# The delta-rule layer's turned keys: products of 32 rows in place of 64-row products over a two-head copy

## The chip, the cores and the metric

The kernel runs on one core of one Trainium2 chip, in float32. The metric is the device time of one launch in microseconds (us). Engines: TensorE (PE, with its weight loads as PEld), VectorE (DVE), ScalarE (ACT), GpSimd (POOL), and SyncE (SP), which here only issues DMAs.

## The reference

The reference is four transformer-like layers, one after the other (attention, gated delta rule, retention, a linear recurrence, each followed by a mixture of experts). The change is in the second one, the delta rule over 8 sequences of 256 tokens. The width of 128 is 4 heads of 32, and the tokens are taken in chunks of 32. What the change touches, cut to its core:

```python
q = silu(causal_dwconv(hidden @ Wq, wq_conv))      # likewise k and v; 4 taps
q, k = l2norm(q), l2norm(k)
v, kb = v * beta[..., None], k * beta[..., None]
# everything in chunks of 32 tokens, per head
inv = -(kb @ swap(k)) * strict_lower
for i in range(1, chunk):
    inv = inv.at[..., i, :].add(einsum('...j,...jk->...k', inv[..., i, :], inv))
inv = inv + eye(chunk)
u, w = inv @ v, inv @ kb
def step(S, xs):                                     # chunk after chunk
    qi, ki, ui, wi = xs
    attn = qi @ swap(ki) * lower_incl
    ui2 = ui - wi @ S
    oi = qi @ S + attn @ ui2
    return S + swap(ki) @ ui2, oi
```

Then come two FIR filters of the values, a gate over the four branches, a norm and an output projection.

## The kernel before

Each layer is a block of its own; inside a block every engine has an instruction list written out by hand in program order, and semaphores ("tallies", `wait_ge` and `then_inc`) set what waits for what. The delta layer is `delta_scan` followed by `delta_gate`. Its data lie as 128 partitions, which are 4 heads times 32, by 2048 columns, which are 8 sequences (b) times 8 chunks (n) times 32; a (b, n) pair is a unit, 64 in all. `kT` holds the turned keys (dimension of the head on partitions, token in columns), `qT` the queries, `kH` the keys turned back, in 32 by 32 blocks.

**Two forms of product.** A product of one head needs only a 32 by 32 block of weights. `products` issues it so, dense: one matmul for each of the 4 heads, on partitions `head(h)`, 32 for a chunk of the 8 sequences. `pair_products` issues it with two heads side by side: the weights are 64 by 64, on partitions `two_heads(i)`, and the two blocks off the diagonal must be zero, so 16 matmuls do for a chunk. Such weights are a copy with the head index e spread out (`kT_heads`, and `inverse`). The copies are made by ScalarE with a scale per partition from `heads` (1 for the heads of parity e, 0 for the others). In the trace every float32 matmul is two records of weight load and two of product.

**The order of `delta_scan`**, by engine:

1. TensorE: gate projection; the convolution of k (`convolve(2, ...)`, 4 groups g of 512 columns into psB); then `pairs(psA, f["kT"], g)`, the products of keys with keys, for the 4 groups; convolutions of v, transposes of windows, the filters, the convolution of q; `pairs(psB, f["qT"], g)`, queries with keys.
2. ScalarE in this phase: for g = 0..3 `silu(0, ...)` writes kT from psB, two more activations write `kT_heads` from psB and signal `split`, then the square of kH of the group before; the fifth turn squares the last group, and a square root follows.
3. VectorE: turns kT into kH by groups, sums the squares (`ssk`), works out the factors `G`, `rk`, `rt`, multiplies psA by `G` (L2757), turns it (L2763), and runs the inversion of the 32 by 32 triangles as 31 pairs of instructions (L2768, L2772). Then it turns the result into r3 (L2786), from which ScalarE makes the two-head copy `inverse` (L2632).
4. The scan over n = 0..7. TensorE: K = keys times state into psK (n above 0), O = queries times state into psO, U = inverse times r into psU, S = kH times u2 into psS, A = attention block times u2 into psO. VectorE: r = vb minus K (L2846), state plus S (L2861); ScalarE copies psU to u2 (L2693). Between these VectorE does side work in program order: evictions of O (`evict`, L2805), the statistics sums, `turn_filtered` at n = 2 and 3 (L2797), `short_sums` at n = 5, 6, 7. I call the steps step 0 to step 7.

Then `delta_gate` begins with a chain of TensorE products (L3044 to L3058).

Of the kernel before, what the change touches and what calls it, by code (L numbers as in the profile page):

```python
# [8 lines left out]
ACT = mybir.ActivationFunctionType  # L9
AX = mybir.AxisListType  # L10

P = 128
# [2333 lines left out]
CH = 32  # L2346
DHEADS = D // CH
UN = N // CH
CPS = SEQ // CH
# [86 lines left out]
def delta_scan(k, f, vpad, w, windows, raw, small, one, sums, r2, r3):  # L2436

    nc = k.nc
    w_in = k.tally("df_w_in")
    scaled, made, convd, silud, spread, moved, fired, firs_in = (  # L2440
        k.tally(f"df_{n}") for n in ("scaled", "made", "convd", "silud", "turned", "moved", "fired", "firs_in"))
# [3 lines left out]
    carried, copied, less, solved, solved_out, read, added, out_done = (  # L2445
        k.tally(f"dt_{n}") for n in ("carried", "copied", "less", "solved", "solved_out", "read", "added", "out_done"))
    cols, rows = w["cols"], w["rows"]
    cleared, cons = k.tally("df_raw_read"), k.tally("dg_cons")
    split, inverted, powered, vsummed, dsquared, dsummed = (
        k.tally(f"ds_{n}") for n in ("split", "inverted", "powered", "vsummed", "dsquared", "dsummed"))  # L2450
    inverse = windows[:].rearrange("p n c -> p (n c)").rearrange("p (u e c) -> p u e c", e=2, c=CH)
    unit_heads = lambda t, b, n, i: t[2 * CH * i:2 * CH * (i + 1), b * CPS + n, :, :].rearrange("p e c -> p (e c)")
    wc = w["conv"][:].rearrange("p (i j c) -> p i j c", i=3, c=D)
    seqs = lambda t: t.rearrange("p (b s) -> p b s", s=SEQ)
    H = lambda ap: ap.rearrange("p (u d) -> p u d", d=CH)
# [4 lines left out]
    head = lambda h: slice(CH * h, CH * (h + 1))  # L2460
    two_heads = lambda i: slice(2 * CH * i, 2 * CH * (i + 1))
    unit = lambda b, n: slice((b * CPS + n) * CH, (b * CPS + n + 1) * CH)
    with ExitStack() as s:
        sb = lambda n, shape: s.enter_context(nc.sbuf_tensor(f"ds_{n}", shape, F32))
        incl, heads = sb("incl", [P, CH]), sb("heads", [P, 2])
        kT_heads = sb("kT_heads", [P, UN, 2, CH])
        tmp = sb("tmp", [P, 2, CH * CH // 4 + CH])
        state, r, u2 = (sb(n, [P, BATCH, CH]) for n in ("state", "r", "u2"))
        squares = tmp[:].rearrange("p g c -> p (g c)")[:, 0:2 * BATCH * CH].rearrange("p (i b c) -> p i b c", i=2, c=CH)
# [48 lines left out]
        @block.tensor  # L2518
        def _(pe):
            def convolve(i, ps, g):  # L2520
                out, x = seqs(ps[:, g, :]), seqs(part(k.XT, g))
                for late in range(CONV):
                    m = nc.tensor.matmul(out[:, :, late:], wc[:, i, CONV - 1 - late, :], x[:, :, 0:SEQ - late],
                                         start=(late == 0), stop=(late == CONV - 1))
                m.then_inc(convd.sem, 1)

            def pairs(out, right, q):
                for b in (2 * q, 2 * q + 1):
                    for n in range(CPS):
                        for i in range(2):  # L2530
                            m = nc.tensor.matmul(
                                out[two_heads(i), q, (b % 2 * CPS + n) * CH:(b % 2 * CPS + n + 1) * CH],
                                unit_heads(kT_heads, b, n, i), right[two_heads(i), unit(b, n)],
                                start=True, stop=True)
                m.then_inc(multiplied.sem, 1)

            def spread_windows(ps, b):
                for j in range(4):
                    m = nc.tensor.transpose(ps[:, b % 4, j * P:(j + 1) * P], vpad[:, b, LONG * j:LONG * j + P],
                                            k.ident[:])  # L2540
                m.then_inc(spread.sem, 1)

            def filter_half(ps, half):
                for d in range(16 * half, 16 * half + 16):
                    for h in range(DHEADS):
                        m = nc.tensor.matmul(ps[CH * h:CH * (h + 1), d % 16 // 4, d % 4 * P:(d % 4 + 1) * P],
                                             windows[:, :, CH * h + d], k.firs[:, d, h, :], start=True, stop=True)
                m.then_inc(fired.sem, 1)

            def pair_products(out, left, n, right):  # L2550
                for b in range(BATCH):
                    for i in range(2):
                        m = nc.tensor.matmul(out[two_heads(i), b * CH:(b + 1) * CH], unit_heads(left, b, n, i),
                                             right[two_heads(i), b, :], start=b == 0, stop=True,
                                             skip_group_check=True)
                return m

            def products(out, left, n, right, start=None, stop=True):
                for b in range(BATCH):
                    for h in range(DHEADS):  # L2560
                        m = nc.tensor.matmul(out[head(h), b * CH:(b + 1) * CH], left[head(h), unit(b, n)],
                                             right[head(h), b, :], start=b == 0 if start is None else start, stop=stop,
                                             skip_group_check=True)
                return m

            pe.wait_ge(*w_in.at(16 * DELTA_LOADS))
            for g in range(4):
                m = nc.tensor.matmul(psA[:, g, :], w["Wxg"][:], part(k.XT, g), start=True, stop=True)
            m.then_inc(gates.sem, 1)
            pe.wait_ge(*scaled.at(1))  # L2570
            for g in range(4):
                convolve(2, psB, g)
            pe.wait_ge(*gout.at(1))
            for g in range(4):
                pe.wait_ge(*split.at(g + 1))
                pairs(psA, f["kT"], g)

            pe.wait_ge(*scaled.at(2))
            convolve(0, psB, 0)
            convolve(0, psB, 1)  # L2580
            pe.wait_ge(*opened.at(4))
            for g in (0, 1):
                if g:
                    convolve(0, psB, 2)
                pe.wait_ge(*silud.at(4 + g + 1))
                spread_windows(psA, 2 * g)
                spread_windows(psA, 2 * g + 1)
            convolve(0, psB, 3)
            for g in (2, 3):
                pe.wait_ge(*silud.at(4 + g + 1))  # L2590
                spread_windows(psB, 2 * g)
                spread_windows(psB, 2 * g + 1)
            pe.wait_ge(*firs_in.at(64))
            pe.wait_ge(*moved.at(8))
            filter_half(psA, 0)
            filter_half(psB, 1)

            pe.wait_ge(*scaled.at(3))
            pe.wait_ge(*kept.at(1))
            for g in range(4):  # L2600
                convolve(1, psA, g)
            pe.wait_ge(*kept.at(2))
            for g in range(4):
                pe.wait_ge(*silud.at(8 + g + 1))
                pairs(psB, f["qT"], g)

            for n in range(CPS):
                if n:
                    pe.wait_ge(*added.at(n))
                    pair_products(psK, kT_heads, n, state).then_inc(carried.sem, 1)  # L2610
                    if n > 1:
                        pe.wait_ge(*copied.at(n - 1))
                    products(psO[n % 2], f["qT"], n, state, stop=False)
                pe.wait_ge(*split.at(4 + n + 1))
                pe.wait_ge(*less.at(n + 1))
                pair_products(psU, inverse, n, r if n else at(f["vb"], 0)).then_inc(solved.sem, 1)
                pe.wait_ge(*solved_out.at(n + 1))
                if n < CPS - 1:
                    products(psS, f["kH"], n, u2).then_inc(read.sem, 1)
                if n == 0:  # L2620
                    pe.wait_ge(*opened.at(8))
                products(psO[n % 2], f["attn"], n, u2, start=False if n else None).then_inc(out_done.sem, 1)

        @block.scalar
        def _(act):
# [23 lines left out]
            for g in range(5):  # L2649
                if g < 4:  # L2650
                    silu(0, seqs(part(f["kT"], g)), psB, g)
                    for e in range(2):
                        m = nc.scalar.activation(kT_heads[:, 16 * g:16 * g + 16, e, :], H(psB[:, g, :]), ACT.Silu,
                                                 scale=heads[:, e:e + 1])
                    m.then_inc(split.sem, 1)
                if g:
                    act.wait_ge(*turned.at(1 + g))
                    nc.scalar.activation(part(r3, g - 1), part(f["kH"], g - 1), ACT.Square).then_inc(squared.sem, 1)
# [219 lines left out]
            output_sums(CPS - 1)  # L2878
    gates.close(1); gout.close(1); turned.close(5); squared.close(8); made.close(2)
    rooted.close(2); asked.close(2); sig.close(1)  # L2880
    split.close(4 + CPS); inverted.close(2); cleared.close(1); powered.close(14)
    vsummed.close(1); dsquared.close(CPS - 1); dsummed.close(CPS)


# [633 lines left out]
```

## Time and profile before

| | |
|---|---|
| median of 3 runs | 1330.14 us (1330.45, 1330.14, 1320.05) |
| profiled execution | 1328.31 us, of which its span is 1326.6 us |
| granted TensorE clock, mean | 0.894 |
| PE, PEld, DVE, ACT, POOL busy | 1098.2, 804.9, 800.2, 534.7, 377.4 us |
| `delta_scan` in that span | about 345 to 483 us |
| `delta_gate` | about 483 to 552 us |

Busy shares are means over all layers; the two stretches of the delta layer are read by themselves. The granted clock is a share of TensorE's full rate of 2.4 GHz; in any one moment it is 1.0 or 0.5 (1.2 GHz). A matmul's own duration is its latency; how densely matmuls follow one another is read from when the first and the last of a group start.

### The profile page before, as it was taken

The numbers are of one execution on the slowest core, as the hardware profiler recorded it, in microseconds if no ns is written. First come the engines' busy times: TensorE is split into PE (matmuls) and PEld (weight loads), VectorE is DVE, ScalarE is ACT, GpSimd is POOL, SyncE is SP. The second block draws the span as 40 slices with busy tenths as digits, with TensorE's granted clock in tenths as the row PEclk, the third lists the DMA queues.
The fourth block names the chain that finished last, engine by engine and source line by source line (L and its number), as shares of the span: only waits on it lengthen the run. The fifth ranks groups of instructions, "written<-read, shape, count | busy, mean of one in ns | idle before, by whom it ended". The sixth has DMA issues, their size and how long they took to land. (4 is left out here: it accounts for less than half of the span.)

```text
span 1326.6 us, 28735 instructions
## 1 busy us (share of the span) xinstructions
PE 1098.2 (83%) x9623; PEld 804.9 (61%) x9631; DVE 800.2 (60%) x2789; ACT 534.7 (40%) x1167; POOL 377.4 (28%) x515
## 2 busy tenths in 40 slices
PE   8999887884998883789976858886878989899892
PEld 4655555674466851446644414553756979889791
DVE  6566245344588669635566785556962767767423
ACT  4365632474553331222222113332213656658481
POOL 2444405343101530000000014660024444534351
PEclk9899978898998566899987976998987999999996
DMA  1200439222000049049917064652902212031212
GB/s 48 55 33 3 152 132 381 62 65 76 1 2 2 4 151 367 1 114 184 318 53 258 2 211 123 147 141 68 362 25 69 70 35 69 22 72 43 62 47 64
DMA packets 112895, 135.88 MB, mean 102 GB/s; under 512 B 16899, under 2 KB 78422, under 8 KB 112096
## 3 DMA queue, kind: packets, MB, share of 16 engines
q1 hardware_dynamic: 100160, 119.26, 29.1%
q0 software_dynamic: 12592, 14.79, 4.4%
q8 instruction: 80, 1.31, 0.4%
q14 instruction: 63, 0.52, 0.1%
HBM read 67.92 MB, written 69.32 MB: 103 GB/s over the span
## 5 line engine op out<-in xcount | busy, mean ns | idle before, releaser
L2116 PE MATMUL m_psY<-large,m_hT 128*128 (+2 forms) x992 | 139.2, 284 | 0.0
L2116 PEld LDWEIGHTS m_psY<-large,m_hT 128*128 128x128 f32 x992 | 126.7, 191 | 0.1
L2035 POOL DMA_INDIRECT rows<-m_ys,m_slot x93 | 90.7, 975 | 113.6 <-DVE m_slot L2271 102.9
L567 DVE TENSOR_REDUCE at_peaks<-at_ps 128x3 f32<-128x384 f32 x128 | 65.4, 552 | 47.6 <-PE at_ps L330 47.6
L479 ACT ACTIVATE at_PT<-at_ps,at_bias 128x384 f32<-128x384 f32 x128 | 67.3, 577 | 50.2 <-PE at_ps L340 50.1
L2172 ACT ACTIVATE m_hT<-m_psH 128x512 f32<-128x512 f32 x124 | 73.7, 594 | 30.1 <-PE m_psH L2098 29.7
L1480 POOL IOTA sl_late<- 64x1024 f32 x2 | 2.0, 984 | 284.8 <-POOLq L682 284.7
L126 PE MATMUL ln_idle<-blank,ident 128*128 128x512 f32 x112 | 54.1, 640 | 27.5 <-PEq L891 14.8
L274 POOL TENSOR_SCALAR_AFFINE_SELECT at_PT<-at_PT 128x256 f32<-128x256 f32 x128 | 54.9, 430 | 74.0 <-ACT at_PT L479 70.0
L2098 PE MATMUL m_psH<-m_xT,large 128*128 128x128 f32 x512 | 67.6, 275 | 0.0
L2184 ACT ACTIVATE m_ys<-m_psY,m_weight 128x144 f32<-128x144 f32 x124 | 47.3, 381 | 42.7 <-PE m_psY L2116 38.3
L2098 PE MATMUL m_psH<-m_xT,m_up 128*128 128x128 f32 x480 | 63.7, 276 | 0.0
L2098 PEld LDWEIGHTS m_psH<-m_xT,large 128*128 128x128 f32 x512 | 63.5, 194 | 0.0
L2098 PEld LDWEIGHTS m_psH<-m_xT,m_up 128*128 128x128 f32 x480 | 59.8, 195 | 0.0
L126 PEld LDWEIGHTS ln_idle<-blank,ident 128*128 128x128 f32 x112 | 22.4, 206 | 54.8 <-issue 54.8
L1377 ACT ACTIVATE pe_sg<-pe_psG 128x512 f32<-128x512 f32 x36 | 21.5, 597 | 69.6 <-PE pe_psU L1345 69.6
L2165 ACT ACTIVATE m_xT<-m_psX 128x128 f32<-128x128 f32 x124 | 32.8, 264 | 41.0 <-PE m_psX L2085 41.0
L1047 PE MATMUL m_psH<-m_xT,m_up 128*128 128x128 f32 x280 | 41.7, 295 | 8.8 <-issue 8.4
L327 PE MATMUL at_ps<-large,at_QA 32*128 32x256 f32 x256 | 46.0, 433 | 3.4 <-ACT at_PT L479 2.3
L1353 PEld LDWEIGHTS pe_psD<-m_wd,pe_hid 128*128 128x128 f32 x288 | 37.5, 191 | 18.5 <-DVE pe_hid L1398 13.8
L981 POOL DMA_INDIRECT pair_sums<-m_ys,m_dest x35 | 34.4, 983 | 44.2 <-ACT m_ys L1106 30.8
L337 PE MATMUL at_ps<-at_QA,large 32*128 32x256 f32 x256 | 44.8, 425 | 2.5 <-ACT at_PT L479 2.3
(709 smaller groups left out, 2780.5 us busy)
## 6 DMA issues: line engine op xcount, KB each, us to landing
rows<-blank SPq DMA_DIRECT2D x16, 2448.0 KB, 21.0
m_xs<-rows SPq DMA_DIRECT2D x124, 76.5 KB, 2.0
pair_rows<-blank SPq DMA_DIRECT2D x1, 8320.0 KB, 25.7
large<-in_L_attn_firs SPq DMA_DIRECT2D x4, 2048.0 KB, 19.1
large<-comb_rows SPq DMA_DIRECT2D x64, 128.0 KB, 5.1
se_wu<-in_L_ffn_up SPq DMA_DIRECT2D x32, 192.0 KB, 2.6
W2T<-in_L_ffn_down_turned SPq DMA_DIRECT2D x1, 4096.0 KB, 12.3
large<-in_L_ffn_up SPq DMA_DIRECT2D x4, 1024.0 KB, 8.2
```

Of the source, the lines that this page charges most:

```text
L126: nc.tensor.matmul(idle[:], k.ident[:], k.blank[:, 0:512], start=True, stop=True)
L274: nc.gpsimd.affine_select(out=diag(PT[:, v % PRING]), in_=diag(PT[:, v % PRING]), compare_op=ALU.is_ge, fill=0.0, base=0, pattern=[[0, 2], ...
L327: return nc.tensor.matmul(psS[:, u % TILES, P:CAUSAL], QA[rows, g, keys(b, 1)], KA[rows, g, b * SEQ:(b + 1) * SEQ], start=False, stop=True ...
L337: return nc.tensor.matmul(psT[:, v % TRING, 0:SEQ], KA[rows, g, keys(b, 0)], QA[rows, g, b * SEQ:(b + 1) * SEQ], start=True, stop=True, sk ...
L479: nc.scalar.activation(PT[:, v % PRING, :, :].rearrange("p x c -> p (x c)"), psT[:, v % TRING, 0:CAUSAL], ACT.Exp, bias=k.at_bias[:, v % H ...
L567: nc.vector.tensor_reduce(peaks[:, b % 2, n, :], psS[:, u % TILES, 0:CAUSAL].rearrange("p (x c) -> p x c", c=P), AX.X, ALU.max).then_inc(r ...
L1047: m = nc.tensor.matmul(psH[b][:, c * P:(c + 1) * P], up[b][:, c * P:(c + 1) * P], xT[b][:], start=True, stop=True)
L2035: pool.indirect_dma_start(k.rows[(layer + 1) % 2], bass.IndirectOffsetOnAxis(slot[:, q:q + 1], 0), ys[:, q, :], None, bounds_check=E3 * N ...
L2098: m = nc.tensor.matmul(psH[b][:, c * P:(c + 1) * P], w[:, c * P:(c + 1) * P], xT[b][:], start=True, stop=True)
L2116: m = nc.tensor.matmul(psY[b][:, 0:wide], hT[b][:, c * P:(c + 1) * P], w, start=(c == 0), stop=(c == C - 1))
L2172: nc.scalar.activation(hT[b][:], psH[b][:], ACT.Silu).then_inc(silu_done.sem, 1)
L2184: nc.scalar.activation(ys[:, q, 0:WIDE], psY[b][:, 0:WIDE], ACT.Copy, scale=weight[:, j % XRING:j % XRING + 1]).then_inc(y_out.sem, 1)
```

## The change

`kT_heads` is given up, with the 8 activations that filled it. Three users change. `pairs` issues, for each unit, 4 matmuls of 32 by 32 weights straight from kT in place of 2 of 64 by 64: 256 in place of 128, twice. Step K of the scan uses `products` in place of `pair_products`: 32 matmuls in place of 16, in 7 steps. And `pairs` on the keys waits for `silud`, the signal of kT itself, not for `split`. The inverse stays two heads side by side. The outputs lie where they lay, and the sums over a head have the same 32 terms (the 64-row form added 32 products with zero).

```diff
--- before.py
+++ after.py
@@ -2463,7 +2463,6 @@
     with ExitStack() as s:
         sb = lambda n, shape: s.enter_context(nc.sbuf_tensor(f"ds_{n}", shape, F32))
         incl, heads = sb("incl", [P, CH]), sb("heads", [P, 2])
-        kT_heads = sb("kT_heads", [P, UN, 2, CH])
         tmp = sb("tmp", [P, 2, CH * CH // 4 + CH])
         state, r, u2 = (sb(n, [P, BATCH, CH]) for n in ("state", "r", "u2"))
         squares = tmp[:].rearrange("p g c -> p (g c)")[:, 0:2 * BATCH * CH].rearrange("p (i b c) -> p i b c", i=2, c=CH)
@@ -2527,11 +2526,10 @@
             def pairs(out, right, q):
                 for b in (2 * q, 2 * q + 1):
                     for n in range(CPS):
-                        for i in range(2):
+                        for h in range(DHEADS):
                             m = nc.tensor.matmul(
-                                out[two_heads(i), q, (b % 2 * CPS + n) * CH:(b % 2 * CPS + n + 1) * CH],
-                                unit_heads(kT_heads, b, n, i), right[two_heads(i), unit(b, n)],
-                                start=True, stop=True)
+                                out[head(h), q, (b % 2 * CPS + n) * CH:(b % 2 * CPS + n + 1) * CH],
+                                f["kT"][head(h), unit(b, n)], right[head(h), unit(b, n)], start=True, stop=True)
                 m.then_inc(multiplied.sem, 1)
 
             def spread_windows(ps, b):
@@ -2572,7 +2570,7 @@
                 convolve(2, psB, g)
             pe.wait_ge(*gout.at(1))
             for g in range(4):
-                pe.wait_ge(*split.at(g + 1))
+                pe.wait_ge(*silud.at(g + 1))
                 pairs(psA, f["kT"], g)
 
             pe.wait_ge(*scaled.at(2))
@@ -2607,11 +2605,11 @@
             for n in range(CPS):
                 if n:
                     pe.wait_ge(*added.at(n))
-                    pair_products(psK, kT_heads, n, state).then_inc(carried.sem, 1)
+                    products(psK, f["kT"], n, state).then_inc(carried.sem, 1)
                     if n > 1:
                         pe.wait_ge(*copied.at(n - 1))
                     products(psO[n % 2], f["qT"], n, state, stop=False)
-                pe.wait_ge(*split.at(4 + n + 1))
+                pe.wait_ge(*split.at(n + 1))
                 pe.wait_ge(*less.at(n + 1))
                 pair_products(psU, inverse, n, r if n else at(f["vb"], 0)).then_inc(solved.sem, 1)
                 pe.wait_ge(*solved_out.at(n + 1))
@@ -2649,10 +2647,6 @@
             for g in range(5):
                 if g < 4:
                     silu(0, seqs(part(f["kT"], g)), psB, g)
-                    for e in range(2):
-                        m = nc.scalar.activation(kT_heads[:, 16 * g:16 * g + 16, e, :], H(psB[:, g, :]), ACT.Silu,
-                                                 scale=heads[:, e:e + 1])
-                    m.then_inc(split.sem, 1)
                 if g:
                     act.wait_ge(*turned.at(1 + g))
                     nc.scalar.activation(part(r3, g - 1), part(f["kH"], g - 1), ACT.Square).then_inc(squared.sem, 1)
@@ -2878,7 +2872,7 @@
             output_sums(CPS - 1)
     gates.close(1); gout.close(1); turned.close(5); squared.close(8); made.close(2)
     rooted.close(2); asked.close(2); sig.close(1)
-    split.close(4 + CPS); inverted.close(2); cleared.close(1); powered.close(14)
+    split.close(CPS); inverted.close(2); cleared.close(1); powered.close(14)
     vsummed.close(1); dsquared.close(CPS - 1); dsummed.close(CPS)
 
 
```

On TensorE, from the products of keys with keys (`pairs` into psA) the row before the change and the one after:

```order
L2531 MATMUL ds_psA<-de_kT,ds_kT_heads 64x32 x128
```

```order
L2530 MATMUL ds_psA<-de_kT 32x32 x256
```

Nothing around this row is in another place; its count doubles and its weights come from kT. On TensorE the first rows of steps 1 and 2 of the scan, in the order K, O, U, S, A, first before:

```order
L2553 MATMUL ds_psA<-ds_state,ds_kT_heads 64x32 x16
L2561 MATMUL ds_psB<-ds_state,large 32x32 x32
L2553 MATMUL ds_psA<-ds_r,de_windows 64x32 x16
L2561 MATMUL ds_psA<-ds_u,de_kH 32x32 x32
L2561 MATMUL ds_psB<-ds_u,large 32x32 x32
L2553 MATMUL ds_psA<-ds_state,ds_kT_heads 64x32 x16
```

and after:

```order
L2559 MATMUL ds_psA<-ds_state,de_kT 32x32 x32
L2559 MATMUL ds_psB<-ds_state,large 32x32 x32
L2551 MATMUL ds_psA<-ds_r,de_windows 64x32 x16
L2559 MATMUL ds_psA<-ds_u,de_kH 32x32 x32
L2559 MATMUL ds_psB<-ds_u,large 32x32 x32
L2559 MATMUL ds_psA<-ds_state,de_kT 32x32 x32
```

The order stands; K has the form of O, S and A, and only U has the 64-row form. On ScalarE, the end of the key groups (from the kT of g = 2), before:

```order
L2628 ACTIVATE de_kT<-ds_psB 128x512
L2653 ACTIVATE ds_kT_heads<-ds_psB,ds_heads 128x16x32 x2
L2658 ACTIVATE de_r<-de_kH 128x512
L2628 ACTIVATE de_kT<-ds_psB 128x512
L2653 ACTIVATE ds_kT_heads<-ds_psB,ds_heads 128x16x32 x2
L2658 ACTIVATE de_r<-de_kH 128x512 x2
```

and after:

```order
L2626 ACTIVATE de_kT<-ds_psB 128x512
L2652 ACTIVATE de_r<-de_kH 128x512
L2626 ACTIVATE de_kT<-ds_psB 128x512
L2652 ACTIVATE de_r<-de_kH 128x512 x2
```

The squares now come right behind the writes of kT. VectorE's, GpSimd's and SyncE's lists are the same.

## Rows read from the trace of the kernel before

**Rows 1.** Busy time and granted clock (PEclk) of stretches: products with keys, scan, gate

```profile
core 0: us, PE busy (x) PEld busy (x) DVE busy (x) ACT busy (x) POOL busy (x), PEclk, DMA share, GB/s
362.50:370.00 7.50, 7.50 (x257) 7.49 (x256) 5.02 (x15) 7.21 (x12) 0.00 (x0) 1.00 0.01 2
...
419.60:420.00 0.40, 0.40 (x16) 0.40 (x16) 0.40 (x2) 0.40 (x2) 0.00 (x0) 1.00 0.00 0
...
423.40:482.00 58.60, 46.66 (x1735) 43.78 (x1728) 43.58 (x95) 19.26 (x38) 32.03 (x31) 0.50 0.01 4
483.00:488.00 5.00, 5.00 (x6) 2.15 (x7) 4.67 (x9) 1.67 (x2) 0.00 (x0) 0.50 0.78 283
488.50:497.00 8.50, 8.50 (x21) 3.72 (x20) 1.43 (x2) 4.03 (x5) 0.00 (x0) 1.00 1.03 372
```

**Rows 2.** Timeline from the last key group to the inversion (start, us, engine, line)

```profile
362.51 7.66 PE L2531 MATMUL ds_psA<-de_kT,ds_kT_heads 64*64 64x32 f32 x256
362.62 0.60 ACT L2628 ACTIVATE de_kT<-ds_psB 128x512 f32<-128x512 f32 x1 [1.14 <-PE ds_psB L2523]
363.11 1.26 ACT L2653 ACTIVATE ds_kT_heads<-ds_psB,ds_heads 128x512 f32<-128x512 f32 x2
363.25 0.71 DVE L2733 STREAM_TRANSPOSE de_kH<-de_kT 128x512 f32<-128x512 f32 x1 [1.05 <-ACT de_kT L2628]
364.25 1.16 ACT L2658 ACTIVATE de_r<-de_kH 128x512 f32<-128x512 f32 x2
...
365.53 0.68 DVE L2738 TENSOR_REDUCE de_ssk<-de_r 128x16 f32<-128x512 f32 x1
...
369.86 1.28 DVE L2757 TENSOR_TENSOR de_r<-ds_psA,de_G 128x512 f32<-128x512 f32 x2
...
373.13 1.25 DVE L2757 TENSOR_TENSOR de_r<-ds_psA,de_G 128x512 f32<-128x512 f32 x2
```

**Rows 3.** Timeline from the products of queries with keys to step 0

```profile
409.52 7.66 PE L2531 MATMUL ds_psB<-large,ds_kT_heads 64*64 64x32 f32 x256
...
414.90 3.67 DVE L2786 STREAM_TRANSPOSE de_r<-de_T 128x2048 f32<-128x2048 f32 x1
...
419.56 1.51 PE L2553 MATMUL ds_psA<-large,de_windows 64*64 64x32 f32 x32 [2.39 <-ACT de_windows L2632]
421.11 0.37 ACT L2693 COPY ds_u<-ds_psA 128x256 f32<-128x256 f32 x1 [0.80 <-PE ds_psA L2553]
...
421.54 1.08 PE L2561 MATMUL ds_psA<-ds_u,de_kH 32*32 32x32 f32 x64 [0.47 <-ACT ds_u L2693]
...
422.41 1.06 PE L2561 MATMUL ds_psA<-ds_u,large 32*32 32x32 f32 x64
```

**Rows 4.** Timeline of steps 2 and 3, where VectorE comes last

```profile
436.36 1.07 PE L2561 MATMUL ds_psA<-ds_state,large 32*32 32x32 f32 x64 [0.22 <-DVE large L2805]
...
441.24 3.71 DVE L2797 STREAM_TRANSPOSE large<-de_raw 128x1024 f32<-128x1024 f32 x2
...
444.81 0.39 DVE L2846 TENSOR_TENSOR ds_r<-large,ds_psA 128x256 f32<-128x256 f32 x1
```

**Rows 5.** Timeline of step 5: state, K, O, r, U

```profile
456.82 0.42 DVE L2861 TENSOR_TENSOR ds_state<-ds_state,ds_psA 128x256 f32<-128x256 f32 x1 [2.06 <-PE ds_psA L2561]
...
457.54 1.92 PE L2553 MATMUL ds_psA<-ds_state,ds_kT_heads 64*64 64x32 f32 x32
...
459.39 1.07 PE L2561 MATMUL ds_psB<-ds_state,large 32*32 32x32 f32 x64
459.50 0.42 DVE L2846 TENSOR_TENSOR ds_r<-large,ds_psA 128x256 f32<-128x256 f32 x1 [2.26 <-PE ds_psA L2553]
...
460.39 1.92 PE L2553 MATMUL ds_psA<-ds_r,de_windows 64*64 64x32 f32 x32
```

**Rows 6.** Timeline of step 6 (A's last records) and of step 7's r

```profile
464.85 0.42 PE L2561 MATMUL ds_psB<-ds_u,large 32*32 32x32 f32 x11 [0.25 <-issue]
...
475.02 0.42 DVE L2846 TENSOR_TENSOR ds_r<-large,ds_psA 128x256 f32<-128x256 f32 x1
```

**Rows 7.** Timeline of the gate: what VectorE waits for

```profile
495.37 3.29 DVE L2946 STREAM_TRANSPOSE de_T<-dg_psL 128x512 f32<-128x512 f32 x4 [7.47 <-PE dg_psL L3058]
```

## The prediction

> **What bounds the kernel now.** The table of busy time names TensorE first, but it is a mean over all the layers, and the chain that ended last reaches back only over the last norm, so neither prices this change. I read three other views: the timeline of the delta layer, engine by engine, for what ends last before each step; the waits written behind the rows; and the windows, for the granted clock. The delta layer lies alone in its block, about 345 to 483 us for the scan, and the gate behind it starts only when it is done, so what it gains or loses at its end goes into the total one for one.
>
> Inside it the chain changes hands. From the last key group on it is VectorE's: squares, factors, multiplication of psA, inversion [rows 2], then the turning of the inverse [rows 3]. TensorE's 256 records of keys with keys run from 362.51 to 370.17, and VectorE takes psA at 369.86 after a chain of its own; there is no wait for a product on that row [rows 2]. Step 0 waits for the turned inverse and its copy: TensorE idles 2.39 us before it [rows 3]. In the scan the chain is state, K, r, U, S, state, with VectorE's side work in between. Every clock row from 423.4 to 482 reads 0.5, where the rows of the two dense product groups before it read 1.0 [rows 1].
>
> **The products of 32 rows, one by one.** In the half-clock stretch, K has 32 records and takes 459.39 minus 457.54 = 1.85 us to the start of the next group, 58 ns for each [rows 5]. A dense group has 64 records for the same work: S to A in step 0 is 422.41 minus 421.54 = 0.87 us, 14 ns each [rows 3]. In step 5, O to U is 460.39 minus 459.39 = 1.00 us [rows 5], of which I put the 0.13 above 0.87 down to the change of form. So four small products flow in the time in which one large one does, and twice as many records still take half the time. At full clock, 256 records of the 64-row form take 7.5 us, 29 ns each, half of 58 [rows 1]; the 32-row form is not shown there. Its bounds are 14 ns (nothing gained from the clock) and 7 ns (halved as the large form is), so 512 records take 3.6 to 7.2 us in place of 7.6. I take the middle, 5 us.
>
> One rule speaks against this. The Trainium skill (TensorE: Matmul & The Clock Gate, "Wait — 56ns, not 53.3ns?") says that start to start never falls below about 25 ns however small the matmul. By it a dense K would take 64 times 25 = 1.6 us, and a group of 512 would take 12.8 us. The trace's 14 ns on tiles of 32 by 32 is below that floor, so for tiles on different rows of the array the measurement decides.
>
> **Keys, first part.** Removed: 8 activations, in pairs of 1.26 us [rows 2]. Three pairs lie before the last kT, while TensorE's convolution of the last group ends only at 362.6, so they were covered; ScalarE even waited 1.14 us for it [rows 2]. The last pair is not. Now: kT 362.62 to 363.22, pair to 364.37, two squares to 365.41, last sum at 365.53. After: the square of g = 2 starts at 363.1; the last square needs kH of g = 3, which VectorE turns from 363.25 to 363.96 [rows 2], so it runs from about 364.03 to 364.65, and the last sum starts at about 364.7. Gain **0.83 us**, not 1.26, because the turning is late next. The rest of VectorE's chain to 369.86 is as before. It would now meet psA at 369.0; the products of the first group are then done at any of the bounds (362.5 plus 7.2 is 369.7 even for the last group, which is needed at 372.3 [rows 2]). The square root's function load on ScalarE moves with the squares.
>
> TensorE is done with the keys 2.6 us sooner (5 us in place of 7.6; 0.4 to 4 by the bounds). What follows there, convolutions, windows, filters, queries with keys, is not the last wait of anything: it ends at 417.2, 2.39 us before step 0 [rows 3]. It costs and brings nothing by itself; the queries' products end at about 409.5 minus 2.6 plus 5 = 412. The inversion has VectorE alone, and starts and ends 0.83 us sooner, r3 at about 417.7 in place of 418.6.
>
> **Step 0, a loss.** TensorE now idles some 6.8 us before U of step 0, in place of 2.39. The clock is still 1.0 at 419.6 to 420.0 [rows 1], so the first half of U ran full; 1.51 us in all, where U at half clock takes 1.92 [rows 3, 5]. After the longer idle time I expect it at half from the start: **0.41 us lost**, with 0 as the other end. No run shows the idle time at which it falls.
>
> **Steps 1 to 4, nothing.** Step 2: O waits for VectorE's eviction, not for K, and starts at 436.36; r follows that same eviction, and U follows both [rows 4]. Steps 3 and 4: `turn_filtered` holds VectorE for 3.71 us from 441.24, and r comes at 444.81, straight behind it, with no wait for K; step 4 repeats it [rows 4]. Step 1 has the turning of the values in the same place. K sooner by 1 us meets a busy VectorE in all four.
>
> **Steps 5 and 6, the gain.** Here VectorE waits: 2.26 us before r of step 5 [rows 5]. Now: state done at 457.24, K 457.54, O 459.39, U 460.39. After: A's last records are followed by K in the same form, so K starts at about 457.37; K 0.87, O 1.00, U at 459.24. r starts at 457.37 plus about 1.1 = 458.5 and is done by 458.9, before U. Gain **1.15 us**. Step 6 has the same form, with K and O giving 0.98 back for certain; its A has a gap in issue with 11 records after it at 464.85 [rows 6] that delays K today and may go or grow (0 to 0.5 us either way): **1.0 us**. Step 7: `short_sums` keep VectorE busy right up to r at 475.02, on which no wait is written [rows 6], so it only moves with the others. From there VectorE's sums and the last eviction are the chain to the end.
>
> **The gate.** It starts earlier and is TensorE's: VectorE waits 7.47 us for its products [rows 7]. The clock there was 0.5 up to 488 and 1.0 from 488.5 [rows 1], some 5.2 us after its first product. If it rises as late after the start, nothing changes; a microsecond sooner or later is worth 0.5 us. I take 0, with 0.8 either way.
>
> **Sum.** 0.83 minus 0.41 plus 1.15 plus 1.0 = 2.6 us sooner; with the ends, 1.0 to 4.2. On the profiled execution 1328.31 minus 2.6 = 1325.7; the median of the runs lies 1.8 us above that execution, so 1330.14 minus 2.6 gives **1327.5 us**. Within 1% is about what a measurement of this kernel can't tell from no change, and 2.6 us is 0.2%; one of the three runs, 10 us below the other two, shows more than that by itself.
>
> **Rivals.**
> 1. *The gain is spent before it reaches the end.* VectorE's side work or the gap in issue takes up what K gives in steps 5 and 6, as it does in steps 2 to 4. For: K, O and A are all alike now, 64 records each, so TensorE takes 576 records of weights and products where it took 512 in a step. Against: the 2.26 us wait. Then 0.83 minus 0.41 stays, about 1330 us.
> 2. *Slower: the clock rises late in the gate.* TensorE's scan is sparser now by 7 times 1 us and idles longer before. If the clock stays at half until the gate's chain ends at 495.4, the work between 488.3 and there takes twice its time, 7.1 us more. With the gains 1330.14 minus 2.6 plus 7.1 = 1334.6 us. It decides against the change when the rise is over 5.2 us later than now, relative to the start. Against: the gate's products are eight dense groups of 512 columns in both kernels.
> 3. *Spacing by product, not by tile.* If the 32-row products of `pairs` at full clock cost as much each as the 64-row ones, 29.5 ns, keys take 15.1 us, queries too, and the queries end at 409.5 plus 7.5 plus 15.1 = 432.1 where step 0 needs them at 419.6: 12.5 us lost, less 2.2 from the scan, 1340 us. Against: 14 ns in the same array at half its clock. The skill's floor of 25 ns on the same page would put the end of the queries at 409.5 plus 5.2 plus 12.8 = 427.5, some 8 us late.
> 4. *The runs lie elsewhere.* One run of before took 1320.05. If two of the runs of after do so as well, the median is about 1318, with the same mechanism.
>
> **How the numbers follow.** Forecast 0.62; rival 1 0.17; rival 2 0.08; rival 3 0.03; rival 4 0.10. The range takes in the forecast with its ends (1326 to 1329.2), rivals 1 and 4, and part of 2: 1318 to 1333 us. Faster by over 1% means below 1316.8: half of rival 4 and a little for the unforeseen, 0.07. Slower by over 1% means above 1343.4: 0.03, out of rivals 2 and 3 joined. Within 1%: 0.90.
>
> **What would show it.** In the profile after: the last sum of squares some 2.2 us after the last kT starts, not 2.9; the keys' products within 3.6 to 7.2 us; no instruction of L2757 waiting for a product; U of step 0 spread over 1.9 us; K's records 14 ns apart in the scan; in steps 5 and 6 U starting 2 us after the state is ready, not 3.1; steps 2, 3 and 4 as long as before; the scan 2 to 3 us shorter. Wrong would be: a K that takes 1.6 us or more, a granted clock of 0.5 before 410, or steps 5 and 6 as long as now.

## The result: slower by 1%, and where the time went

The changed kernel takes 1341.98 us (median of 4 runs, 1340.68 to 1345.5), the kernel before 1329.28 us (4 runs); the ratio is 1.0101, 95% interval 1.0057 to 1.0145. Forecast were 1327.5 us and a range up to 1333. The profiled execution took 1341.34 us, its span is 1339.6 us, 13.0 over the span before; the mean granted clock is 0.885.

Up to the keys' products the two traces agree to 0.1 us. These are the lines of the timeline of after that answer to [rows 2]:

```profile
362.58 2.33 PE L2530 MATMUL ds_psA<-de_kT 32*32 32x32 f32 x250
...
364.73 0.69 DVE L2732 TENSOR_REDUCE de_ssk<-de_r 128x16 f32<-128x512 f32 x1
...
366.91 1.30 PE L2530 MATMUL ds_psA<-de_kT 32*32 32x32 f32 x128 [1.99 <-issue]
...
369.07 1.28 DVE L2751 TENSOR_TENSOR de_r<-ds_psA,de_G 128x512 f32<-128x512 f32 x2
...
370.63 1.93 PE L2530 MATMUL ds_psA<-de_kT 32*32 32x32 f32 x128 [2.43 <-issue]
...
374.09 0.33 PE L2530 MATMUL ds_psA<-de_kT 32*32 32x32 f32 x6 [1.53 <-issue]
374.34 9.50 PE L2522 MATMUL ds_psB<-XT,de_conv 128*128 128x512 f32 x16
374.46 0.69 DVE L2751 TENSOR_TENSOR de_r<-ds_psA,de_G 128x512 f32<-128x512 f32 x1 [1.52 <-PE ds_psA L2530]
```

The first 250 records of product run in 2.33 us, 9 ns apart. Then TensorE stands for 2 us, with no engine named as the one it waits for ("issue"), runs exactly 128 records, stands, runs 128, stands. A record of product has a record of load beside it, so 128 of them are 256 instructions. The group ends at 374.4 where the 64-row form ended at 370.2, and VectorE, which has its factors 0.8 us sooner than before (369.07 against 369.86), waits 1.52 us for the last of them. So the inversion begins at 377.26 instead of 376.54.

The clock adds to it. Windows of after (columns as in [rows 1]):

```profile
362.60:364.90 2.30, 2.30 (x251) 2.20 (x251) 1.45 (x3) 1.93 (x4) 0.00 (x0) 1.00 0.03 7
...
368.20:370.60 2.40, 0.01 (x1) 0.00 (x0) 2.08 (x7) 1.35 (x2) 0.00 (x0) 0.66 0.00 0
370.60:372.50 1.90, 1.87 (x128) 1.79 (x128) 1.90 (x2) 0.00 (x0) 0.00 (x0) 0.50 0.03 9
...
374.40:380.00 5.60, 5.60 (x10) 2.47 (x9) 4.85 (x10) 0.00 (x0) 0.00 (x0) 0.57 0.00 0
...
380.00:390.00 10.00, 10.00 (x37) 5.29 (x36) 8.81 (x17) 5.01 (x8) 0.00 (x0) 1.00 0.01 2
```

From 370.6 to 374 the granted clock is at 0.5, and for most of the stretch to 380 it still is (mean 0.57), where before it was 1.0; the first two convolutions of v take 9.50 us where they took 7.09. With 4.2 us from the keys and 2.4 from the clock, TensorE reaches the queries' products at 416.17, 6.65 us late. They show the same pattern (timeline of after, for [rows 3]):

```profile
416.17 1.49 PE L2530 MATMUL ds_psB<-large,de_kT 32*32 32x32 f32 x152
...
419.68 1.67 PE L2530 MATMUL ds_psB<-large,de_kT 32*32 32x32 f32 x128 [2.02 <-issue]
...
423.13 1.93 PE L2530 MATMUL ds_psB<-large,de_kT 32*32 32x32 f32 x128 [1.78 <-issue]
...
426.59 1.61 PE L2530 MATMUL ds_psB<-large,de_kT 32*32 32x32 f32 x104 [1.52 <-issue]
...
428.13 1.49 PE L2551 MATMUL ds_psA<-large,de_windows 64*64 64x32 f32 x24
```

Each run of 128 begins 3.45 to 3.5 us after the one before it. The whole takes 12.0 us, step 0 can't start before 428.13, and the 2.39 us in which TensorE used to wait for it are gone: it starts 8.6 us late. In the scan the gaps come inside K and O, for instance in steps 1, 3, 5 and 7 of after:

```profile
437.88 0.33 PE L2559 MATMUL ds_psB<-ds_state,large 32*32 32x32 f32 x8 [2.07 <-issue]
...
450.92 0.94 PE L2559 MATMUL ds_psA<-ds_state,de_kT 32*32 32x32 f32 x55
453.52 0.36 PE L2559 MATMUL ds_psA<-ds_state,de_kT 32*32 32x32 f32 x9 [1.66 <-issue]
453.64 1.09 PE L2559 MATMUL ds_psB<-ds_state,large 32*32 32x32 f32 x64
454.76 1.92 PE L2551 MATMUL ds_psA<-ds_r,de_windows 64*64 64x32 f32 x32
...
471.85 0.42 PE L2559 MATMUL ds_psB<-ds_state,large 32*32 32x32 f32 x10 [1.79 <-issue]
...
486.41 0.37 PE L2559 MATMUL ds_psA<-ds_state,de_kT 32*32 32x32 f32 x10 [1.80 <-issue]
```

From step 0 to the gate's first product (494.83) the stretch takes 66.7 us, where it took 63.4. Not every gap costs something. Measured from the start of one U to the next, the ways to steps 2, 3 and 4 take 8.56, 7.96 and 7.94 us, as before (8.56, 7.99, 7.95), though K is broken off for 1.66 us in step 3: VectorE is later still there. The loss comes from U of step 0 to U of step 1 (10.11 us in place of 9.24) and from U of step 4 to U of step 5 (9.50 in place of 7.09).

The gate starts 11.8 us late and gives 1.3 us back; the layer's last write is 10.5 us late. The other 2.5 of the 13.0 us come in later layers that the change doesn't touch.

A queue of the DMA engines that brings instructions, q8, is in the page. For the whole of after, for the stretch from 362 to 375 us, and when the DMA engines were busy in that stretch (40 slices of 0.325 us):

```profile
q8 instruction: 86, 1.41, 0.4%
```

```profile
q8 instruction: 3, 0.05, 1.5%
```

```profile
DMA  0000000100000000002000000000010000000000
```

Before, it had 80 packets and 1.31 MB; a packet is 16 KB. The change adds 368 matmuls, 1472 instructions, and 6 packets, so a packet holds some 250 instructions. In the 13 us of the keys' products 3 packets came. The other queue of instructions, q14, has 63 packets in both, so q8 is TensorE's. That made the theory for the experiments: **TensorE's instructions arrive in pieces of 256, about one per 3.5 us when asked for one after another, with two in hand at the start.** The rival is that the 32-row products are slow in themselves, in the array or by the clock.

The DMA records of the traces bear the theory out packet by packet. In after the three packets start at 364.48, 367.94 and 371.74 us and land 0.96, 1.27 and 0.93 us later; TensorE goes on at 366.91, 370.63 and 374.09, which is 1.4 to 1.5 us behind each landing. In the delta layer (345 to 495 us) of the nine kernels here there are 61 gaps in issue of 0.4 us or more, and each ends 1.2 to 1.6 us after a q8 packet has landed. Where one run of 128 follows another in the keys and queries of after, the next packet starts 1.0 to 1.2 us after a run has begun, at either clock. These parts, 1.1 us to the start of a packet, 1.0 for the packet and 1.4 to the next record, add up to the 3.5 us; the time is a round trip for each packet, and not only the packet's own.

### The profile page after: what moved, and what is told of

Same layout as the page of the kernel before. It is cut to its first block and busy times, and to the rows that moved or that the text cites. A ratio compares the mean times of both kernels' runs of the same rounds, so it can differ in the third digit from the quotient of the medians.

```text
span 1339.6 us, 30207 instructions
## 1 busy us (share of the span) xinstructions
PE 1096.7 (82%) x10367; PEld 797.8 (60%) x10367; DVE 801.5 (60%) x2789; ACT 530.8 (40%) x1159; POOL 379.1 (28%) x515
## 5 line engine op out<-in xcount | busy, mean ns | idle before, releaser
L567 DVE TENSOR_REDUCE at_peaks<-at_ps 128x3 f32<-128x384 f32 x128 | 65.4, 552 | 47.7 <-PE at_ps L330 47.7
```

Source lines behind the costliest of these rows:

```text
L567: nc.vector.tensor_reduce(peaks[:, b % 2, n, :], psS[:, u % TILES, 0:CAUSAL].rearrange("p (x c) -> p x c", c=P), AX.X, ALU.max).then_inc(r ...
```

## The experiments

The absolute start of the delta layer differs by up to 12 us between the executions, so I compare two stretches of TensorE's timeline in each: from the first product of keys to the first U of step 0, and from there to the gate's first product. Each is read from one profiled execution. Where nothing in a stretch is changed, the first repeats within 0.2 us (before, e1, e5) and the second within 1 us (before, e2, e6, e7). Those of e1 to e4 ran on one chip (kernel before there: 1328.35 us, 27 runs), e5 to e7 on another (kernel before: 1349.84 us, 23 runs); ratios are taken within a chip.

| kernel | keys to step 0, us | step 0 to gate, us | ratio to before (95%) |
|---|---|---|---|
| before | 57.1 | 63.4 | |
| after | 65.6 | 66.7 | 1.0101 (1.0057 to 1.0145) |
| e1, K alone dense | 57.0 | 67.6 | 1.0017 (0.9988 to 1.0046) |
| e2, `pairs` alone dense | 65.4 | 63.9 | 1.0102 (1.007 to 1.0134) |
| e3, after, interleaved | 58.7 | 66.2 | 1.0054 (1.002 to 1.0088) |
| e4, after, 8 columns | 66.0 | 67.1 | one run, no ratio |
| e5, K dense, half of O | 56.9 | 61.2 | one run, no ratio |
| e6, e3 with K two heads | 58.5 | 63.1 | 1.003 (0.9991 to 1.0068) |
| e7, before, late copy | 56.2 | 62.9 | 1.0015 (0.9982 to 1.0048) |

**e1, one part alone: K of the scan.**

```diff
-                    pair_products(psK, kT_heads, n, state).then_inc(carried.sem, 1)
+                    products(psK, f["kT"], n, state).then_inc(carried.sem, 1)
```

> The kernel before with K of the scan dense (32-row products from kT) and nothing else changed; kT_heads and both `pairs` stay two heads side by side. Theory A (delivery of instructions: TensorE's instructions come in pieces of 16 KB, 256 instructions or 128 records of product, one piece per 3.5 us or so once the two in hand are used up; a step of the scan now takes 576 in place of 512): step 0 starts as before at 419.6, the scan from step 0 to the gate's first product takes 66.5 to 67 us in place of 63.4, total 3 us over before. Theory B (the 32-row form itself is slow in the array or brings the clock down; no effect of the count of instructions): K flows at 14 ns per record, the scan is 2 us shorter as I forecast, total 2 us under before.

The scan lost 4.2 us, a little more than theory A said, and the stretch ahead of it nothing. Timeline of e1 in steps 3 and 5:

```profile
440.10 0.94 PE L2561 MATMUL ds_psA<-ds_state,de_kT 32*32 32x32 f32 x55
442.44 0.37 PE L2561 MATMUL ds_psA<-ds_state,de_kT 32*32 32x32 f32 x9 [1.40 <-issue]
442.57 1.09 PE L2561 MATMUL ds_psB<-ds_state,large 32*32 32x32 f32 x64
...
461.59 0.42 PE L2561 MATMUL ds_psB<-ds_state,large 32*32 32x32 f32 x10 [2.08 <-issue]
```

K flows 14 to 15 ns per record as forecast, and in step 3 breaks off for 1.4 us after 55 of its 64. That gap costs nothing, since VectorE is later; the one in step 5's O does, and 3 of the 4.2 us are lost between U of step 4 and U of step 5. A step now has K, O, S and A at 64 records and U at 32, 576 instructions with the loads, in place of 512. The scan's stretch is the evidence; over the whole kernel 2.3 us lie within the interval.

**e2, the other part alone: both `pairs`.** The change's `pairs` with K left as it was.

```diff
...
-                        for i in range(2):
+                        for h in range(DHEADS):
                             m = nc.tensor.matmul(
-                                out[two_heads(i), q, (b % 2 * CPS + n) * CH:(b % 2 * CPS + n + 1) * CH],
-                                unit_heads(kT_heads, b, n, i), right[two_heads(i), unit(b, n)],
-                                start=True, stop=True)
+                                out[head(h), q, (b % 2 * CPS + n) * CH:(b % 2 * CPS + n + 1) * CH],
+                                f["kT"][head(h), unit(b, n)], right[head(h), unit(b, n)], start=True, stop=True)
...
-                pe.wait_ge(*split.at(g + 1))
+                pe.wait_ge(*silud.at(g + 1))
```

> The kernel before with both `pairs` dense and K of the scan left in the two-head form (ScalarE still writes kT_heads). Theory A: gaps of about 2 us in issue every 128 records, the keys' products take 11 to 12 us, the queries' 11 to 12 us, step 0 starts 8.5 us later than before, the scan itself takes 63 to 64 us as before; total 8 to 10 us over before. Theory B gives the same total, but with the records spread evenly. Rival C (the loss of after comes from the scan): step 0 as before, total within 2 us of before.

It has the whole loss ahead of step 0 (8.4 us) and none in the scan beyond 0.4, with the records in runs of 250, 128, 128 and 6 between gaps of 2.07 to 2.25 us. So the two parts of the change cost separately, each where it stands, and rival C is out.

**e4, a quarter of the array's work, the same instructions.**

```diff
+                            first = (b % 2 * CPS + n) * CH
...
-                                out[head(h), q, (b % 2 * CPS + n) * CH:(b % 2 * CPS + n + 1) * CH],
-                                f["kT"][head(h), unit(b, n)], right[head(h), unit(b, n)], start=True, stop=True)
+                                out[head(h), q, first:first + 8], f["kT"][head(h), unit(b, n)],
+                                right[head(h), (b * CPS + n) * CH:(b * CPS + n) * CH + 8], start=True, stop=True)
```

> The kernel after, but each product of `pairs` computes only the first 8 of its 32 columns (the other columns are left out, so the attention blocks and the inverse are not the reference's); the same number of instructions with a quarter of the columns. Theory A: nothing changes, keys 11 to 12 us, queries 11 to 12 us with the gaps at the same places, step 0 at 427 to 429. Theory B: the products follow one another faster, keys and queries in 3 to 5 us each, step 0 at 419.

As theory A said. Timeline of e4:

```profile
362.38 2.29 PE L2531 MATMUL ds_psA<-de_kT 32*32 32x8 f32 x250
366.69 1.89 PE L2531 MATMUL ds_psA<-de_kT 32*32 32x8 f32 x128 [2.02 <-issue]
370.42 1.89 PE L2531 MATMUL ds_psA<-de_kT 32*32 32x8 f32 x128 [1.83 <-issue]
373.87 0.28 PE L2531 MATMUL ds_psA<-de_kT 32*32 32x8 f32 x6 [1.56 <-issue]
374.08 2.93 PE L2522 MATMUL ds_psB<-XT,de_conv 128*128 128x512 f32 x3
```

The runs have the same counts, and start within 0.3 us of those of after; a quarter of the columns saves nothing, not even in the first 250 records. The time of `pairs` doesn't depend on how many columns the array computes; the loads of weights are the same in e4.

**e3, the same instructions, in another order.** The convolutions of 3.4 us and 16 instructions are put between the groups of products.

```diff
...
+            pe.wait_ge(*scaled.at(2))
             for g in range(4):
                 pe.wait_ge(*silud.at(g + 1))
                 pairs(psA, f["kT"], g)
-
-            pe.wait_ge(*scaled.at(2))
-            convolve(0, psB, 0)
-            convolve(0, psB, 1)
+                if g == 1:
+                    convolve(0, psB, 0)
+                if g > 1:
+                    convolve(0, psB, 1, (0, 1) if g == 2 else (2, 3))
...
-            for g in range(4):
-                convolve(1, psA, g)
-            pe.wait_ge(*kept.at(2))
-            for g in range(4):
-                pe.wait_ge(*silud.at(8 + g + 1))
-                pairs(psB, f["qT"], g)
+            for g in range(5):
+                if g < 4:
+                    convolve(1, psA, g)
+                if g == 0:
+                    pe.wait_ge(*kept.at(2))
+                else:
+                    pe.wait_ge(*silud.at(8 + g))
+                    pairs(psB, f["qT"], g - 1)
```

> The kernel after, with the same TensorE instructions in another order: the keys' groups 2 and 3 stand behind parts of the convolution of v, and each group of queries' products behind the next group of the convolution of q. A group of products is one piece of instructions, a convolution group is 16 instructions in 3.4 us. Theory A: the convolution's time covers the delivery, no gap over 0.5 us is left in either `pairs`, the clock stays at 1.0 to about 415, step 0 starts at 419 to 420; the scan keeps its loss of 3.3 us; total 2 to 4 us over before, some 8 to 9 us under after. Theory B: the products take as long wherever they stand, step 0 starts at 427 or later, total as after.

Timeline of e3, TensorE at the keys and at the queries:

```profile
362.46 2.33 PE L2531 MATMUL ds_psA<-de_kT 32*32 32x32 f32 x250
366.80 0.26 PE L2531 MATMUL ds_psA<-de_kT 32*32 32x32 f32 x6 [2.00 <-issue]
366.98 3.68 PE L2522 MATMUL ds_psB<-XT,de_conv 128*128 128x512 f32 x8
370.59 1.29 PE L2531 MATMUL ds_psA<-de_kT 32*32 32x32 f32 x128
371.81 1.98 PE L2522 MATMUL ds_psB<-XT,de_conv 128*128 128x512 f32 x4
373.72 1.14 PE L2531 MATMUL ds_psA<-de_kT 32*32 32x32 f32 x110
...
402.78 1.29 PE L2531 MATMUL ds_psB<-large,de_kT 32*32 32x32 f32 x128
404.00 3.68 PE L2522 MATMUL ds_psA<-XT,de_conv 128*128 128x512 f32 x8
407.61 1.29 PE L2531 MATMUL ds_psB<-large,de_kT 32*32 32x32 f32 x128
...
412.44 1.49 PE L2531 MATMUL ds_psB<-large,de_kT 32*32 32x32 f32 x153
416.23 1.46 PE L2531 MATMUL ds_psB<-large,de_kT 32*32 32x32 f32 x103 [2.31 <-issue]
```

A group behind a convolution runs its 128 records with no gap over 0.2 us, the clock stays at 1.0 (windows 366.9 to 410), and 6.8 of the 8.5 us ahead of step 0 come back. I had expected the gaps all gone, and was wrong twice: the first two groups need 256 records where 250 were in hand, so 6 records still wait 2.00 us, and the last two groups of queries stand together. The first of these matters: VectorE waits 2.61 us for the keys' last group (375.45), of which the gap is 2.00 and the convolutions ahead of the group the rest; the inversion starts 1.7 us later than before, and step 0 at 421.20, not 419 to 420. That is the 1.7 us that stay lost. The scan keeps its loss of 2.7 us. Timed, e3 is 7 us over before, with an interval of 2.7 to 11.7; from the first product of keys to the layer's last write its profiled execution is 3.4 us over, which the interval takes in. Its runs go from 1326.38 to 1342.98.

**e5, the dense K with the instructions of a step back at 512** (the edit is shown against e1).

```diff
-                    products(psO[n % 2], f["qT"], n, state, stop=False)
+                    products(psO[n % 2], f["qT"], n, state, stop=False, sequences=BATCH // 2)
```

> The kernel with only K of the scan dense, and the products O (queries times state) of every step computed for 4 of the 8 sequences; the other four are left out, so the output is wrong there. A step has 512 instructions again, as before, with K dense. Theory A (one piece of 256 instructions per 3.5 us): the gaps of 1.3 to 2.1 us in issue inside K and O go, what is left is 0.5 us at most; from the start of step 0 to the gate's first product 60 to 62 us, where before has 63.4 and K dense with the whole of O 67.6. Theory B (the dense K, or its change of form, is what stalls): the gaps stay at K and the stretch takes 66 us or more.

The gaps inside K and O are gone in all seven steps, and the stretch takes 61.2 us, 2.2 under before and 6.4 under e1. My half microsecond was too strict: in steps 5 and 6, where nothing else holds TensorE up, gaps of up to 1.25 us are left in A, so even 512 instructions are near the limit there. Timeline of e5, step 3 and the largest gap:

```profile
451.00 1.06 PE L2561 MATMUL ds_psA<-ds_state,de_kT 32*32 32x32 f32 x64
451.85 0.63 PE L2561 MATMUL ds_psB<-ds_state,large 32*32 32x32 f32 x32
454.83 1.92 PE L2553 MATMUL ds_psA<-ds_r,de_windows 64*64 64x32 f32 x32 [2.35 <-DVE ds_r L2846]
...
473.07 0.37 PE L2561 MATMUL ds_psB<-ds_u,large 32*32 32x32 f32 x10 [1.25 <-issue]
```

In step 3 VectorE is last again, as before. How much of the 2.2 us is K's and how much the missing half of O's, this run doesn't separate. The clock has a part as well: the gain is in steps 5 and 6, and from 468 to 471 us the granted clock of e5 is 0.89 and from 471 to 473 it is 0.77, where before it was 0.5 throughout the scan. What decides between the theories is that the gaps in K and O went with the instructions, and that q8 has 80 packets again, as before, where e1 has 82.

**e6, e3 with K in the two-head form again**, and kT_heads written late:

```diff
...
-                    products(psK, f["kT"], n, state).then_inc(carried.sem, 1)
+                    pair_products(psK, kT_heads, n, state).then_inc(carried.sem, 1)
...
+            for e in range(2):
+                nc.scalar.activation(kT_heads[:, :, e, :], H(f["kT"]), ACT.Copy, scale=heads[:, e:e + 1])
```

> Dense `pairs` in the interleaved order and K of the scan back in the two-head form; ScalarE writes kT_heads late, in two copies from kT. Theory A: the keys keep the gap of 2 us before their last piece, step 0 starts at 420 to 421.5 as in the interleaved kernel; the scan has 512 instructions a step and takes 63 to 64 us to the gate again, no gap over 0.8 us; total 0 to 2 us over before, 3 to 5 under the interleaved one. If the scan's loss came with the interleaving or the keys and not with K, the scan stays at 66 us.

The scan is back at 63.1 us with no gap in issue over 0.4 us, the keys keep their 2.00 us. So the scan's loss is K's.

**e7, the one gain that needs no dense product.**

```diff
                 if g < 4:
                     silu(0, seqs(part(f["kT"], g)), psB, g)
+                if g < 3:
                     for e in range(2):
                         m = nc.scalar.activation(kT_heads[:, 16 * g:16 * g + 16, e, :], H(psB[:, g, :]), ACT.Silu,
                                                  scale=heads[:, e:e + 1])
                     m.then_inc(split.sem, 1)
...
             nc.scalar.activation(small["rt"][:], small["ssk"][:], ACT.Sqrt).then_inc(rooted.sem, 1)
+            for e in range(2):
+                m = nc.scalar.activation(kT_heads[:, 48:64, e, :], H(part(f["kT"], 3)), ACT.Copy,
+                                         scale=heads[:, e:e + 1])
+            m.then_inc(split.sem, 1)
```

> The kernel before with one move on ScalarE: the last group of kT_heads is copied from kT behind the squares and the square root, not ahead of the squares. No instruction of TensorE changes. It keeps the one gain of my forecast that needs no dense product: the last sum of squares, and with it the inversion and step 0, 0.8 us sooner relative to the last convolution of k; TensorE's last group of keys is due at 368.2 and finds its copy ready at 367.6. Everything else as before, total 0.8 us under before, which the timing can't tell from no change. A rival, that the late copy holds up the last group of keys, gives a wait of TensorE of up to 1 us there and nothing at step 0.

Timeline of e7:

```profile
367.91 7.66 PE L2531 MATMUL ds_psA<-de_kT,ds_kT_heads 64*64 64x32 f32 x256
368.01 0.60 ACT L2628 ACTIVATE de_kT<-ds_psB 128x512 f32<-128x512 f32 x1 [1.14 <-PE ds_psB L2523]
368.51 0.62 ACT L2659 ACTIVATE de_r<-de_kH 128x512 f32<-128x512 f32 x1
...
370.05 0.69 DVE L2743 TENSOR_REDUCE de_ssk<-de_r 128x16 f32<-128x512 f32 x1
...
371.49 1.32 ACT L2663 ACTIVATE ds_kT_heads<-de_kT,ds_heads 128x512 f32<-128x512 f32 x2
```

The products run on without a break, the last sum comes 2.04 us after the last kT starts (2.91 before), and step 0 is 0.9 us sooner. The ratio of 1.0015 holds no change and can't confirm 0.8 us. None of the kernels here is measurably faster than before.

## Why the prediction was wrong, point by point

- **Price of a 32-row product**: 14 ns at half clock, 7 to 14 at full. Measured 9 ns at full clock (250 in 2.33 us). Right for as long as instructions are at hand. Starts 9 ns apart also go against the 25 ns floor of the Trainium skill (TensorE: Matmul & The Clock Gate, "Wait — 56ns, not 53.3ns?"), so that weighing stood.
- **From the price to the group, the step that failed.** "So 512 records take 3.6 to 7.2 us in place of 7.6": measured 11.8 us for the keys, 12.0 for the queries. I carried a rate read from groups of 64 to groups of 512. The 64-row form takes 29.5 ns per record, 3.8 us per 256 instructions, and that is just slower than the delivery; halving the time per instruction halved nothing. The trace before had a sign of it, the gap "issue" with 11 records behind it [rows 6], which I priced as 0 to 0.5 us either way and asked no cause of: it ends 1.4 us after a q8 packet landed (463.44), like the gaps of after.
- **Keys, first part**: the sum of squares was due at 364.7 and came at 364.73, VectorE met psA at 369.07 (369.0). Right, and then lost to a wait of 1.52 us that I had excluded.
- **TensorE ahead of step 0 is not the last wait**: wrong. It had 2.39 us of cover and was done 11.0 us late, so it set step 0, 8.6 us late.
- **Step 0, clock**: U did run at half clock, but not for my reason. In after TensorE doesn't idle ahead of U at all, where I had 6.8 us, and e1 also took 1.92 us for it behind an idle time of only 2.31 us, so my link to a longer idle time isn't borne out. That U ran at half clock as forecast is luck. The clock's real cost was elsewhere, 2.4 us in the convolutions behind the gaps; e3, without most of the gaps, has it back at 1.0.
- **Steps 1 to 4 nothing, 5 and 6 a gain of 2.15**: right for steps 2, 3 and 4, where VectorE covers even the gaps. Step 1 lost 0.9 us and step 5 lost 2.4, for the most part by a gap inside O (2.07 and 1.79 us). The gain of a dense K may be there (e5), but K's 64 added instructions a step cost more: 3.3 us over the scan in after, 4.2 in e1.
- **Gate**: I allowed 0.8 us either way; it gave 1.3 back.
- **The sum**: its own ends (0.41 for the clock, 0.5 for step 6, 0.8 for the gate) give 1.3 to 4.3 us, not 1.0 to 4.2. That is small beside the 8.6 us ahead of step 0, which the sum put at nothing.
- **Rivals.** Rival 3 named the time, 1340 us, with 12.5 us at step 0, and a chance of 0.03. Its mechanism, the array spacing small products like large ones, is refuted by the first 250 records (9 ns) and by e4; the place and nearly the size were right, for another reason. Rival 1 counted the instructions (576 against 512) and then priced them as lost gain only, never as a loss. Rivals 2 and 4 did not occur.

The 2.5 us that after loses behind the delta layer call for no cause. From the layer's last write to the end of the span before takes 774.9 us and after 777.4, and e1 to e4, with the same code there, take 775.2 to 781.5. What stays open is what sets the round trip of 3.5 us, how large the gain of a dense K is when instructions are at hand, and why the timed loss of e2 (9 to 18 us) is a little over the 9.2 us that its delta layer shows.

## What to carry to other kernels

Count instructions, not only their time: a change that splits a product into smaller ones must be held against how fast instructions arrive, here 256 per 3.5 us with about 500 in hand, in every stretch longer than that. If a stretch has work of few long instructions beside it, put the short ones between them: the same instructions in another order gave 6.8 of 8.5 us back. And an idle time marked "issue" in a dense stretch is worth a question before the change: the gap of 0.25 us in A ahead of step 6 was the same limit. The count of packets on the instruction queue, before and after, and where they land, answers it from the trace alone: 2 packets more in e1, 4 in e2, 6 in after.

## What the runs showed of the hardware

Products of 32 by 32 at the full granted clock follow one another at 9 ns, and no faster with 8 columns than with 32 (2.29 us and 2.33 us for 250 records). TensorE's instructions come by DMA in packets of 16 KB, and runs of exactly 128 records of product with as many loads start 3.45 to 4.0 us apart when nothing else is in between. Each such run starts 1.2 to 1.6 us after a packet has landed. The Trainium skill (Runtime: NRT & Kernel Launch, "Instruction fetch mechanics") states that instructions are streamed in blocks of 16 KB, 256 instructions, with only two held (it also gives 2048 instructions for TensorE's store, which would be eight), and that the fetch is hidden behind the dispatch. The trace agrees with the blocks and with the two in hand (250 records, then the first gap), and disagrees with the hiding: up to 2.43 us of TensorE's time per block were not hidden. It disagrees with eight blocks in store as well: in after the first gap comes behind 500 instructions.
